# The last rows of maxima and the sums of the third normalization in the other order on VectorE, in a fused decoder layer

## The reference, cut to what matters

```python
x = layernorm(x + attention1(x))           # depthwise conv, position, 16 heads of 16, bf16 softmax
x = layernorm(x + (causal_self(x) + cross(x, ctx)) @ Wp + bp)   # 16 heads of 16, fp32
x = layernorm(ffn(x))
# ffn: y = x + mag * directions[tile] * output_scale         (a routed expert per token)
#      y = (y - mu) / sqrt(var + eps) * gamma + beta          (the "third normalization")
#      and the outer layernorm of y is the fourth ("last") one
```

## Time and profile before

| | |
|---|---|
| median of 3 runs | 2227.47 us (2224.45 to 2228.35) |
| the profiled execution, its own time | 2221.05 us |
| its span in the profile | 2219.3 us |
| mean granted TensorE clock | 0.972 of full speed |
| PE busy | 2093.4 us, 94% of the span |
| DVE busy | 1754.5 us, 79% |
| ACT busy | 1533.8 us, 69% |
| POOL busy | 755.5 us, 34% |

### The profile page before, as it was taken

One profiled execution on the slowest core, in us unless ns is written; L12 is line 12 of the kernel. 1 busy time (PEld: TensorE's weight loads), 2 busy tenths in 40 slices (PEclk: granted clock), 3 DMA queues, 4 the chain that ended last, 5 costly groups with the idle time before them and its releaser, 6 DMA issues.

```text
span 2219.3 us, 39450 instructions
## 1 busy us (share of the span) xinstructions
PE 2093.4 (94%) x13138; PEld 911.5 (41%) x13138; DVE 1754.5 (79%) x4869; ACT 1533.8 (69%) x3361; POOL 755.5 (34%) x802
## 2 busy tenths in 40 slices
PE   5999999999999999999999999999999999989983
PEld 2344334543444434543335433454344533444332
DVE  6957779688987889778897788968888787977754
ACT  2936887478865888458894688747886578846861
POOL 3026521165113650155402653116521353004620
PEclk8899999999999999999999999999999999999995
DMA  3700034000520006100160003400043000610000
GB/s 111 138 10 1 1 67 86 11 2 1 114 49 10 2 20 124 20 11 2 39 124 10 1 1 76 87 11 1 1 96 58 11 1 11 113 30 1 1 11 10
DMA packets 250858, 81.80 MB, mean 37 GB/s; under 512 B 236064, under 2 KB 247328, under 8 KB 250656
## 3 DMA queue, kind: packets, MB, share of 16 engines
q1 hardware_dynamic: 250656, 79.29, 17.6%
HBM read 16.35 MB, written 4.19 MB: 9 GB/s over the span
## 4 chain that ended last, share of the span: by engine, by line
PE 76%; DVE 12%; ACT 8%; issue 3%; DMA 1%; SPq 0%; POOL 0%; DVEq 0%; POOLq 0%; ACTq 0%
PE bank L1738 14%; PE bank L1807 14%; PE bank L1798 10%; PE bank L1421 7%; PE bank L1734 6%; ACT work L772 5%; PE bank L1795 4%; PE bank L1691 4%; DVE work L977 3%; PE bank L1554 3%; PE bank L1541 2%; PE bank L1577 2%; PE bank L1848 2%; PE bank L1767 1%; DVE stats L982 1%
## 5 line engine op out<-in xcount | busy, mean ns | idle before, releaser
L831 ACT ACTIVATE work<-bank 128x512 f32<-128x512 f32 (+3 forms) x1536 | 723.0, 549 | 261.9 <-PE bank L1795 140.5
L1244 DVE TENSOR_REDUCE top_half<-bank 128x1 f32<-128x512 f32 x1024 | 636.4, 683 | 139.7 <-PE bank L1738 138.4
L1738 PE MATMUL bank<-k_c,q_c 32*128 32x512 f32 x2048 | 536.0, 618 | 0.0
L1798 PE MATMUL bank<-q_c,k_c 32*128 32x512 f32 x2048 | 467.4, 624 | 7.4 <-DVE q_c L1270 6.0
L772 ACT ACTIVATE work<-work,neg 128x512 bf16<-128x512 bf16 x512 | 362.7, 716 | 30.6 <-DVE work L977 29.8
L1807 PE MATMUL bank<-work,v_flat 128*32 128x512 f32 (+3 forms) x3072 | 365.0, 551 | 0.6 <-ACT work L831 0.3
L977 DVE TENSOR_SCALAR_CACHE_REDUCE work<-bank 128x512 bf16<-128x512 f32 x512 | 322.3, 685 | 35.2 <-PE bank L1523 25.1
L1241 DVE CUSTOM_DVE_ANT_0 masked<-bank,mask_w 128x384 bf16<-128x384 f32 (+3 forms) x512 | 226.6, 489 | 118.5 <-PE bank L1734 113.9
L654 POOL TENSOR_TENSOR featA<-featA,featB 128x512 f32<-128x512 f32 (+3 forms) x232 | 241.9, 1043 | 225.9 <-ACT featB L844 223.0
L1738 PEld LDWEIGHTS bank<-k_c,q_c 32*128 32x128 f32 x2048 | 210.9, 183 | 159.8 <-DVE top_half L1244 125.7
L615 POOL TENSOR_SCALAR ln_r<-mv 128x4 f32<-128x4 f32 x32 | 9.0, 281 | 748.9 <-DVE mv L986 748.9
(11 more groups left out here) (208 smaller groups left out, 2627.6 us busy)
## 6 DMA issues: line engine op xcount, KB each, us to landing
xT_pad<-xT SPq DMA_DIRECT2D x16, 256.0 KB, 2.9
ctx_sb<-ctxT SPq DMA_DIRECT2D x8, 512.0 KB, 3.4
x_res<-x SPq DMA_DIRECT2D x8, 512.0 KB, 5.0
out<-r_sb SPq DMA_DIRECT2D x8, 512.0 KB, 2.9
work<-work SPq DMA_TRANSPOSE x112, 4.5
qk_sb<-qkT SPq DMA_DIRECT2D x1, 512.0 KB, 4.6
pe_sb<-pe_w SPq DMA_DIRECT2D x1, 256.0 KB, 4.0
v_sb<-vT SPq DMA_DIRECT2D x1, 256.0 KB, 5.0
```

Of the source, the lines that this page charges most:

```text
L831: nc.scalar.activation(pT[:, s % PT_SLOTS, g, q0:S], exp_bank(n)[:, 0:S - q0], ACT.Exp, scale=SCALE).then_inc(pT_ready, 1)
L1244: nc.vector.tensor_reduce(top_half[:, i % 2, g, u // 2, u % 2:u % 2 + 1], scores, AX.X, ALU.max, negate=True).then_inc(slot_out, 1)
L1738: mm(dst, q_c[rows, i, P * t:P * (t + 1)], k_c[rows, i, S * half:S * (half + 1)], start=True, stop=True, tile_position=(GW * g, 0)).then_i ...
L1798: mm(dst, k_c[rows, i, P * u:P * (u + 1)], q_c[rows, i, :], start=True, stop=True, tile_position=(GW * g, 0)).then_inc(sT_mm, 1)
```

## The change

In step 38 of VectorE's program `put_rows` of cross group 3 is done first and `third_sums` behind it. No instruction is added or removed, and no other engine's program is touched.

```diff
@@ -1296,8 +1296,6 @@
                     if prev and m == SPLINE_LEAD:
                         spline(c, sf)
                 for s in range(ALL_STEPS):
-                    if prev and s == LATE_STEP:
-                        third_sums(c, sf)
                     if prev and s == LATE_STEP + 2:
                         third_norm(c)
                     if prev and s == LATE_STEP + 5:
@@ -1316,6 +1314,8 @@
                             outputs(j)
                     for part in end_rows(s) if s >= LATE_STEP else []:
                         put_rows(*part)
+                    if prev and s == LATE_STEP:
+                        third_sums(c, sf)
                     if s == ALL_STEPS - NC:
                         do(nc.vector.tensor_tensor(x_res[:], x_res[:], over_tiles(bp_row), ALU.add))
                     for part in end_outputs(s) if s >= LATE_STEP else []:
```

## The result

The changed kernel takes 2247.43 us (median of 4 runs, 2246.33 to 2248.96) against 2227.39 us before (2224.45 to 2228.35): ratio 1.0094, interval 1.0078 to 1.0109, 20.0 us slower. The direction and the new wait came as forecast, the size did not: 10.5 us were forecast as the likeliest, and 2247.43 lies just over the upper end of the range, 2247.0. The other half of the loss is a term that the forecast had put at nothing, TensorE's clock. The profiled execution took 2248.07 us with a span of 2246.3 us and a mean granted clock of 0.965.

A forecast was written before the change was run, and what follows sets the result against it. TensorE, busy 94% of the span, was taken to bound the kernel. Six batches at 1.66 us (9.96) plus 0.50 in batch 7 gave 10.5 us on 2227.47, so 2237.9 us, range 2232.5 to 2247.

The forecast's parts named there:

- TensorE's clock: Clock may fall behind the new 2.6 us pause at burst 10: 1.2 us each, 8.4 over seven; taken as nothing.
- Steps 1 and 2: Step 38: `put_rows` starts 0.69 us behind the transposes, VectorE idles 2.66; step 40 comes 0.93 us early without its wait.
- Steps 3 to 6: VectorE from `third_sums` through `third_norm` and residual add to `outputs(9)`: sums end 2.66 us late, `outputs(9)` starts at about 549.97.
- The contention: VectorE's residual add against GpSimd's convolution: up to 1.07 us a batch, 5.4 in all, if the phase shifts; taken as nothing.
- Step 7: First product of burst 10 waits 2.6 us for `outputs(9)`, starting 0.75 us after it and 1.93 us later than before.
- Step 8: ScalarE catches up during the new wait, so step 43's scores take 1.14 us instead of 1.41: 0.27 back.
- The sum of the wait: Net delay of 1.66 us in each of batches 1 to 6 and 0.50 in batch 7, 10.5 us in all.
- the third rival: Slower, and the clock falls behind the pause in most of seven batches: 10.5 + 8.4 = 18.9 us, 2246.4; 17%.
- The falls that might go: Existing clock falls in the batches may vanish as later work shifts: 2 x 2.4 = 4.8 us off; taken as nothing.
- "faster" rival: Gain at step 40 is kept if `outputs(9)` is not late: 0.93 us seven times, 6.5 us off, 2221.0; 4%.

The follow-up runs named there:

- the run with ten dummies: Changed kernel with ten dummy matmuls on TensorE between step 42's scores and burst 10, filling the pause: 2234.89 us against 2226.41 for the kernel before, ratio 1.0049.
- the split with the bias add put later: Changed kernel, third normalization's statistics ahead of `put_rows`, gamma and beta behind, bias add in step 42: 2214.12 us, repeated 2219.36; ratios 0.9959, 0.9966 to the kernel before.
- the split alone: Changed kernel with the third normalization's statistics ahead of `put_rows`, gamma multiply and beta add behind: 2224.11 us against 2226.41 for the kernel before, ratio 0.999.
- The run with 1.65 us idle: Changed kernel with four dummy matmuls on TensorE between step 42's scores and burst 10: 2235.55 us against 2226.12 for the kernel before, ratio 1.0035.
- the one with 1.4 us: Changed kernel with VectorE's bias add moved from step 40 to 42, behind the sum of burst 9: 2233.77 us against 2226.41 for the kernel before, ratio 1.0034.
- The control: Kernel before the change with only the bias add moved from step 40 to step 42: 2227.42 us against 2226.12, ratio 1.0001.

## Why the prediction was right in its steps and wrong in its size

- Steps 1 and 2, the wait at step 40 goes and VectorE idles instead: right. `put_rows` starts 0.70 us behind the transposes (0.69 forecast), and step 40 is 0.92 us earlier (0.93).
- Steps 3 to 6, VectorE's chain to the sum of burst 9: right. From `put_rows` to the sum it took 9.56 us, forecast 9.54. The reciprocal deviation stayed hidden, and the bias add took 1.18 us in the same phase with GpSimd. The contention at up to 1.07 us a batch did not come.
- Step 7, the new wait: right, 2.62 us (2.6 forecast), with burst 10 at 11.09 us behind the transposes (10.98). The hand-over took 0.83 us and not 0.75.
- Step 8, 0.27 us back because ScalarE catches up: right where the clock is full. Step 43 takes 1.14 us in batch 4 and in the run with the pause filled.
- The sum of the wait: 1.76 us a batch against 1.66, and 0.65 in batch 7 against 0.50, so 11.2 us in place of 10.5. The run with ten dummies measures it as a whole with 8.5 us by the medians, 11 by the ratio. Nothing of it was taken back in the next batch: in the run with ten dummies the period from batch 1 to batch 2 took 265.13 us without a fall, and 263.30 before.
- What failed is the term "TensorE's clock". I took nothing for it as the likeliest, gave its rival 17%, and priced a fall at 1.2 us, with one stretch per pause. The clock fell behind five of the seven pauses, and there it cost 1.59 to 1.63 us three times and 2.71 and 2.88 in two, 10.4 us in all. The price of 1.2 came from half of a period's excess with two stretches at 0.50, elsewhere in the batch. In one of these VectorE and ScalarE were busy throughout as well; whether that makes a fall cheaper there is not shown. In steps 42 and 43 the half-speed matmuls lengthen the batch one for one: in batch 1 the first product of burst 10 took 0.87 us longer than at full clock, the scores of step 43 0.95 us and the next product 0.88, together 2.70 of the 2.71.
- The reason for taking nothing was the pause of 0.85 us, three times shorter. The nearest row by length was the pause of 2.71 us in the tail, behind which the clock stood at 0.53. What came agrees with it, but it is a weak witness: in the kernel before, the tail's clock was low ahead of that pause too, and full only around it (the pause is 2175.40 to 2178.11):

```profile
2170.00:2175.00 5.00, 5.00 (x16) 2.93 (x15) 0.42 (x1) 0.29 (x1) 0.00 (x0) 0.53 0.00 0
2175.00:2178.00 3.00, 0.41 (x1) 0.00 (x0) 0.00 (x0) 2.53 (x3) 0.00 (x0) 1.00 0.00 0
```

- With the measured falls put in, the sum is 11.2 + 10.4 = 21.6 us, where 20.0 was measured. So what happened is the third rival, slower with the clock fallen as well. That its own working came near, with 18.9 us, is in part luck: it counted seven batches at 1.2 us, and five lost 2.1 us on average.
- The falls that might go, 4.8 us in the other direction: in the profiled execution those of batches 2 and 4 did go, but others came in batches 1, 3, 5 and 6, so the rest of the kernel took some 5 us more (27.0 less 21.7) and not less.
- The Trainium skill's advice (TensorE: Matmul & The Clock Gate, "Why this matters for your kernels": pauses below about 3 us keep the throughput) does not hold here: 2.62 us of idleness were followed by the lower clock in five of six batches of the profiled execution.
- The bound of the "faster" rival, 2.6 us of VectorE's work too much in between, proved to be a recipe. Leaving 2.0 us of it in the idle time ahead of `put_rows` and putting 1.2 behind the sum of burst 9 gave the 0.93 us a batch.

## What to carry to other kernels

When an instruction is moved ahead of a block of work, follow the block to the next thing that the bounding engine needs from that queue: here 4.8 us of sums that had covered an idle 2.6 us pushed the next bank's release past its due time. Put into the idle time as much of the block as fits, and put behind the next due instruction what can wait; the split with the bias add put later beat both orders, and the split alone only matched the order before. A pause on TensorE like the one of 2.6 us here, in a stretch where nothing else bounds the kernel, is to be priced with a fall of the clock behind it, from rows of that length and not from shorter ones.

## What the runs showed of the hardware that was not expected

- The granted clock fell behind an idle time of 2.6 us in five of six batches, behind 1.65 us in two of six, and behind 1.4, 0.85, 0.74 and 0.36 us in none of six each. All these are single profiled executions. The run with 1.65 us idle had the four dummies ahead of the pause, the one with 1.4 us had none, so their order is not a clean one.
- The length of a pause does not decide alone. In batch 6 of all nine profiled executions TensorE pauses 1.34 or 1.35 us in another stage, and in all nine the clock falls beside it, from 0.7 us ahead of its end to 1.8 us behind. The kernel before, timeline of TensorE and busy table:

```profile
1903.84 0.39 PE L1541 MATMUL bank<-k,q 32*128 32x512 bf16 x1 [1.35 <-DVE work L977]
```

```profile
1903.00:1905.00 2.00, 1.16 (x4) 0.37 (x4) 2.00 (x8) 1.20 (x4) 0.59 (x1) 1.00 0.26 54
1905.00:1912.00 7.00, 7.00 (x20) 2.69 (x19) 6.84 (x24) 3.90 (x9) 0.00 (x0) 0.51 0.76 105
```

Falls also come where the profile shows no pause over 0.23 us in the 10 us ahead, as the one at 888 in the earlier trace rows. What separates these places is open.
- The time of one and the same kernel moves with the clock: the kernel before took 2219.44 to 2238.14 us in 29 runs, the fastest with a mean clock of 0.972 and the slowest with 0.963, a spread of 0.8% where four runs had shown 0.2%. The control's profiled execution had a mean clock of 0.963 and a span of 2236.8 us, with no pause ahead of step 40 over 0.85 us in batches 1 to 6, and its kernel's median was that of the kernel before. With 10 to 12 runs against 21 or 29 the intervals were still 3 to 5 us wide to either side. Why the falls elsewhere in the batch are frequent in one execution and rare in the next stays open.
